# Row gathers of a graph kernel's first stage: a long burst replaced by a paced issue, with a shorter lead

## The reference: what is computed

```
h = relu(layernorm(x))                                  # every node
# layer 0, edges (src, dst)
gate = silu(edge_attr @ W1.T + b1) @ W2.T + b2 + logit(type[src], type[dst])
msg  = gate * h[dst] * (cutoff(dist) * node_vec[dst])
agg  = segment_sum(msg, src) / max(segment_sum(node_vec[dst], src), 1e-8)
x    = x + layernorm(h + agg) * gamma + beta
# layer 1
h2   = relu(layernorm(x))
msg  = (relu(h2[src] @ weight1[rel] + bias1) @ weight2[rel]) * norm
x    = x + relu(segment_sum(msg, dst) + bias2)
```

## Time and profile before

| | us |
|---|---|
| median of three runs | 1717.35 |
| time of the profiled execution | 1717.13 |
| its span in the trace | 1715.1 |
| stage one, to the first load of stage two | 860.27 |
| first add into the table | 311.22 |
| last block's `msg` from DVE | 787.86 |

### The profile page before, as it was taken

How to read it: one execution, slowest core, us unless ns; L and a number is a source line. 1 busy time by engine, 2 the same in 40 slices (tenths; PEclk the granted TensorE clock), 3 DMA queues, 4 the chain that set the end, 5 groups by cost and what they waited for, 6 DMA issues and landing times.

```text
span 1715.1 us, 20445 instructions
## 1 busy us (share of the span) xinstructions
PE 1120.0 (65%) x5094; PEld 814.0 (47%) x5094; DVE 1364.2 (80%) x4378; ACT 608.5 (35%) x1423; POOL 1060.7 (62%) x808
## 2 busy tenths in 40 slices
PE   2115888988999988883017888778777777782000
PEld 1003666666777666663005555555555555551000
DVE  4015999999999999993069999999999999992666
ACT  1002544444544454451014444444444444441000
POOL 7772322687866566556645878888888888863000
PEclk9999666666666566665555666666666666666555
DMA  6314999766666666652255656666666666645999
GB/s 177 99 38 146 316 313 322 208 143 164 146 146 151 139 146 137 144 136 38 11 183 160 162 153 154 158 169 156 168 159 155 153 155 163 164 77 152 415 414 375
DMA packets 165336, 298.62 MB, mean 174 GB/s; under 512 B 75034, under 2 KB 91627, under 8 KB 164324
## 3 DMA queue, kind: packets, MB, share of 16 engines
q1 hardware_dynamic: 89172, 253.42, 43.9%
q0 software_dynamic: 68992, 24.64, 16.6%
q10 hardware_dynamic: 7056, 19.27, 2.8%
HBM read 209.28 MB, written 127.50 MB: 196 GB/s over the span
## 4 chain that ended last, share of the span: by engine, by line
POOL 23%; DMA 18%; issue 16%; DVE 15%; PE 14%; ACT 1%; SPq 0%; POOLq 0%; ACTq 0%; DVEq 0%
POOL agg L452 14%; DMA kept_out<-x_mid 7%; PE ps_s L542 6%; POOL agg L490 3%; POOL nodes L411 3%; PE ps_k L616 3%; DMA agg<-y,once 2%; PE ps_m L629 2%; POOL t L480 2%; DVE same L817 2%; DMA agg<-u,once 2%; DMA agg<-ynrm,once 2%; DMA agg<-ysq,once 2%; DVE ynrm L1030 2%; DVE x L1035 2%
## 5 line engine op out<-in xcount | busy, mean ns | idle before, releaser
L490 POOL DMA_INDIRECT agg<-sums,once x196 | 331.0, 1689 | 77.7 <-issue 57.5
L542 PEld LDWEIGHTS ps_s<-msg,same 128*128 128x128 f32 x1856 | 362.0, 300 | 34.1 <-issue 31.8
L542 PE MATMUL ps_s<-msg,same 128*128 128x48 f32 (+1 forms) x1856 | 366.7, 379 | 3.2 <-DVE msg L925 2.2
L411 POOL DMA_INDIRECT nodes<-in_table,dst_all x196 | 195.9, 999 | 159.7 <-DVE hdst L914 100.4
L480 POOL DMA_INDIRECT t<-agg,src_all x196 | 215.5, 1100 | 84.1 <-issue 57.0
L616 PE MATMUL ps_k<-h_t,rw_sb 56*128 56x256 f32 x588 | 124.9, 540 | 134.2 <-issue 97.0
L528 PE MATMUL ps_k<-types_lo,low_hot 128*128 128x392 bf16 x196 | 94.4, 481 | 115.8 <-issue 57.2
L616 PEld LDWEIGHTS ps_k<-h_t,rw_sb 56*128 56x128 f32 x588 | 66.0, 258 | 174.2 <-issue 112.6
L629 PE MATMUL ps_m<-hid,rw_sb 128*64 128x256 f32 x588 | 135.9, 632 | 0.0
L797 DVE SCALAR_TENSOR_TENSOR t<-iota_hi,hi_all,ps_k 128x392 f32<-128x392 f32 x196 | 114.0, 618 | 17.9 <-issue 11.0
L452 POOL DMA_INDIRECT agg<-u,once x48 | 76.6, 1595 | 62.7 <-DMA agg<-in_both 21.9
(11 more groups left out here) (155 smaller groups left out, 2626.1 us busy)
## 6 DMA issues: line engine op xcount, KB each, us to landing
agg<-in_both SPq DMA_DIRECT2D x14, 2758.0 KB
t<-agg SPq DMA_DIRECT2D x49, 784.0 KB
kept<-kept_out SPq DMA_DIRECT2D x49, 404.0 KB
kept_in<-kept SPq DMA_DIRECT2D x49, 404.0 KB
agg<-bias_rows SPq DMA_DIRECT2D x49, 384.0 KB
x_mid<-x SPq DMA_DIRECT2D x49, 384.0 KB
rows<-in_src_rows SPq DMA_DIRECT2D x49, 256.0 KB
rows<-in_dst_rows SPq DMA_DIRECT2D x49, 256.0 KB
```

The lines of the kernel that those rows point to most:

```text
L411: pool.indirect_dma_start(nodes[s][:, t, :], None, table, bass.IndirectOffsetOnAxis(ap=dst_all[:, c:c + 1], axis=0)).then_inc(nodes_in[b % ...
L490: pool.indirect_dma_start(agg1, bass.IndirectOffsetOnAxis(ap=once1[b % LAG1][:, t:t + 1], axis=0), sums1[b % LAG1][:, t, :], None, compute ...
L542: last = mm(ps_s[:, t * width:(t + 1) * width], kept_same[:, at:at + P], m[:, v, :], start=(v == t), stop=(v == a + w - 1))
```

## The change

POOL's burst is cut to blocks 0 to 2. Then come 14 steps; step s issues the gathers of block 3 + s, two once DVE has made block s's one-hot mask (`onehot_done`), and two once it has done `pc_done` of block s. PRERUN becomes 3 + 14 = 17. It also stands in `window0` and in the add loop: 32 iterations now have gathers, and the blocks with windows of two tiles are those below 32 and no longer those below 13.

```diff
-PRERUN = 36
+FIRST = 3
+STEPS = 14
+PRERUN = FIRST + 1 * STEPS
...
-            for b in range(1, PRERUN):
+            for b in range(1, FIRST):
                 gather(b)
+            for step in range(STEPS):
+                for t in range(TILES):
+                    if t == 0:
+                        need(pool, S["hdst_done"], FIRST + step - AHEAD + 1)
+                        need(pool, S["weight_done"], FIRST + step - AHEAD + 1)
+                        pool.wait_ge(S["onehot_done"], step + 1)
+                    if t == 2:
+                        pool.wait_ge(S["pc_done"], step + 1)
+                    gather_tile(FIRST + step, t)
             pool.wait_ge(S["wide_set"], 16 * FILLS)
```

## The result

The changed kernel took 1649.66 to 1666.96 us, median 1657.23, beside 1715.68 to 1723.86 us, median 1717.89, for the kernel before (four runs each). The ratio is 0.9645, 95% interval [0.9588, 0.9702]. The forecast was 1663 us. The profiled execution took 1649.66 us with a span of 1647.6, the lowest of the four.

What follows compares the result with a forecast made beforehand. Stage one ends with POOL's last add, set by the adds' start and 49 iterations. Gain 54 us: 101 from the start, less 59 for 19 more iterations with gathers, 12 back. Forecast 1663 us, range 1645 to 1692.

Steps and rivals of the forecast that it cites:

- The start of the adds: POOL's add loop in stage one: paced gathers let it start at 210 us instead of 311.22.
- the 5 us set aside for a drag of block 0: DVE's first step: allowance for what the short first burst still delays, between 0 and 15 us.
- the other limit: DMA bandwidth during the fills: 58.9 MB at 314 GB/s also puts the adds' start at 210 us.
- that the added waits stand far ahead of `wide_set`: POOL's paced steps: the two added waits hold up only later gathers and the far-off `wide_set`; no cost.
- The iterations: POOL's add loop: 32 iterations with gathers at 13.55 us; without, 10.46 beside DVE or 9.44 after it.
- the Trainium skill's rule: Add loop: gathers locked out by DVE instructions could cost 71 us; 0.16 us a gather was seen, so nothing added.
- narrow windows: DVE's steps in the add loop: two-tile windows save 0.53 us per block for 19 blocks, giving 13.07 us.
- The end of stage one: Stage two's first load: at 806.2 us instead of 860.27, a gain of 54 us.
- the unbroken burst: Early stage one: 69 back-to-back gathers from 50 to 135.6 us, inferred to leave DVE busy only 12 us (the hole).
- the first term: Start of POOL's adds: 101 us gained by starting at 210 us instead of 311.22.
- Rival 1: Early stage one: the hole is not the burst's doing, adds still start at 311.2; 1764 us, slower; chance 0.07.
- The 73 us of the prediction: Early stage one: ACT took up TensorE's centring product, started at 48.05 us and lasting 2, 73 us late.

Runs made afterwards that it cites:

- r2: The changed kernel, unchanged, on a chip where the kernel before took 1720.31 us: 1655.9 us, ratio 0.9622 to the kernel before.
- e2: The changed kernel with a lead of 36 blocks, paced at 8 or 12 gathers a step: 1631.82 us, ratio 1.0018 to the kernel before.
- e5: The changed kernel with the windows of the kernel before (two tiles only for blocks below 13): 1663.28 us, beside 1655.9 for the changed kernel.
- e6: The kernel of e1 (unbroken burst, no pacing) on a chip with the hole: 1713.28 us, ratio 0.9974 to the kernel before.
- e7: The kernel of e2 (lead 36, paced) on a chip with the hole: 1656.22 us, ratio 0.9638 to the kernel before.
- e1: The changed kernel with blocks 0 to 16 gathered in one unbroken burst, no paced steps: 1657.68 us, ratio 1.0206 to the kernel before.
- e10: The kernel of e1 with two POOL memsets after each gather of the burst: 1656.56 us, ratio 1.0211 to the kernel before.
- e9: The changed kernel with 12 POOL memsets between the paced gathers of each step: 1664.27 us, ratio 1.0259 to the kernel before.
- r1: The kernel before, unchanged, run again with a profile: 1721.14 us, ratio 0.9998 to the kernel before.

## Why the prediction was right

**The start of the adds.** Forecast 210 us, measured 204.45 and 203.93: the 5 us set aside for a drag of block 0 were not needed (its step took 12.84 us). The steps of the fills were 12.9 us for 13.0, and the last fill landed about 17 us after its issue. 320 GB/s at a DMA share of 0.97 shows the other limit reached as well. One step of the prediction was wrong and cost nothing: that the added waits stand far ahead of `wide_set`. In r2 the last paced gather goes out at 202.68 us, after the wait for `pc_done` of block 13, and the first add follows it at once; in the first profile the last fill came 1.10 us later. With four gathers a step the two limits meet, which is luck; with twelve in the last step (e2) the gathers are the later one.

**The iterations.** 32 with gathers took 430.9 / 32 = 13.47 us each; forecast 13.55. Gathers in them took 1.05 us each by the profile, so the Trainium skill's rule ("SBUF — State Buffer", two separate sides), by which a gather beside DVE could wait for a whole DVE instruction of up to 0.94 us, priced nothing here that the trace of before had not shown.

**DVE.** With narrow windows (434.97 - 205.57) / 18 = 12.74 us per step, forecast 13.07; with wide ones 13.5, forecast 13.6. DVE was done at 662.7 us for 676. Narrow windows save 0.8 us a step, then, where I had 0.53. The masks were priced rightly: in e5 a block's four take 2.17 us and in r2 1.64. Most of the rest is the matmuls, which had no price: from 250 to 440 us DVE waits for PE's `ps_s` before L923 for 3.6 us in all, over 14 steps, in e5, and not at all in r2. e5 shows the whole as 6 to 7 us of time. There was no wait for rows.

**The end of stage one** was forecast at 806.2 and came at 796.25 and 798.73. Of the 10 us of the first profile, 5.5 are from the start, 3 from the iterations and 2 from the earlier end of DVE. The rest of the span was 854.7 us in r2, as forecast; the 851.4 of the first profile is not explained.

**What was only half right** is the step "so neither DMA load nor a gather as such stalls the engines; what is left is the unbroken burst". On chips with the hole it holds: with the same lead, the hole is there without the pacing and gone with it (e6, r2), it ends soon after the burst (e6), comes in small with 21 us of all but unbroken gathers (e7) and is absent with four to a step (r2). But the same burst costs nothing on two other chips (e1, and the kernel before at 1626 and 1623 us). The sum was right as both the profile and the comparison came with the hole, and that was luck: half of the four chips tried later had none. Without it, to go by the time of the kernel before (92 to 95 us less), the 101 us of the first term are hardly there, and the lead cut is what is left: the changed kernel itself wasn't run there, but e1 and e10, which have its lead, windows and add loop and start their adds at 204.75 and 205.69 us, were 2.1% slower than the kernel before. Rival 1, slower at 1764 us, named the direction of that outcome with a wrong picture: it kept the late start and added the lead's cost. Without the hole the changed kernel's kind starts early, and so, to go by its time, does the kernel before.

The 73 us of the prediction need a note: they are two waits of ACT in a row, 58.09 us for the gate's `ps_m`, which TensorE had done by 48.1, and 21.02 before the centring product's.

**What stays open.** Why chips (or occasions) differ, and by what path gathers delay results of TensorE by 50 to 77 us, no run shows. Loading of instructions, which the prediction could not separate, is not what the engines waited for, as far as a profile shows it: e6 has no packet on the instruction queues between 36 and 110 us, and yet DVE goes on at 67.03 and 99.30 and ACT at 104.16; e1 has six in that stretch. Whether it is the gathers or a POOL that never rests, and whether a slower burst is harmless, was not seen on a chip with the hole (e9 and e10 met the other kind). Nor was two blocks a step, which would be the next to try there.

**A better version.** e2's kernel, lead 36 and paced, is as fast as the changed kernel on a chip with the hole (1656.22 and 1655.9 us) and 26 us faster than its stand-in e1 on one without; against the kernel before it is 3.6% faster or the same. These are comparisons across two chips with the hole (0.9638 and 0.9622 of the kernel before on each). None ran that beats the kernel before on both kinds.

## What to carry to other kernels

A hole that begins and ends with another engine's burst may be caused by it and still not be a property of the program: run the unchanged kernel on another chip, and at another time, before its price goes into a sum. Where a fix (pacing) and a price (a shorter lead) come in one change, find each alone; here the pacing can be had for nearly nothing, and only the shorter lead, at 26 us with its windows, makes the kernel slower where there was nothing to fix. And a paced issue is only as good as its real pauses: waits that are already met leave a burst.

## What the runs showed of the hardware

One and the same kernel (the one before) took 1618 to 1629 us on two chips and 1713 to 1726 on two others, each within 1% over its runs. For the kernel of e1 and e6 the whole difference (55.6 us in time) is there by the second mask (37.16 and 101.74 us). While POOL issued indirect gathers back to back on the latter chips, ACT took up a result of TensorE 50 us (e6), 73 us (the first profile) and 77 us (r1) after it was done, with the DMA engines at a share of 0.12 for part of the time (e6). DVE's waits from 42 to 101 us had nearly the same lengths in these three profiles: 19.3 to 20.0, then 4.4, 5.0 and 20.4 to 21.1 us. What sets them no run shows. A burst of 16 gathers lengthened a step of 13 us by 9 (e7); one of 8 had no effect (r2).
